# Two group-normalised 3x3 convolutions on 1024x1024 images: another chain of statistics between the passes

## The reference, cut to what matters

```
def _gn(v, G=4, eps=1e-5):            # 4 groups of 2 channels, over the whole image
    m, s = mean and var of the group
    return (g - m) / sqrt(s + eps)
x = x + conv3x3(_gn(x), L0_weight, pad=1) + L0_bias
x = x + conv3x3(_gn(x), L1_weight, pad=1) + L1_bias
```

## Time and profile before

| | |
|---|---|
| median of 3 runs | 3917.45 us (3915.92 to 3917.98) |
| profiled execution, own time | 3912.56 us |
| its span, first to last instruction | 3910.9 us |
| TensorE busy | 3472.6 us, 89% |
| ScalarE, VectorE, GpSimd busy | 44%, 37%, 15% |
| mean granted clock of TensorE | 0.969 of full |
| HBM traffic | 805 MB read, 537 MB written, 343 GB/s |

### The profile page before, as it was taken

The page is one execution under the profiler, slowest core; times in us unless marked ns, Lnnn a source line. Parts: engine busy times, 40 slices in busy tenths (PEclk is TensorE's granted clock), DMA queues, the critical chain, the costliest instruction groups (busy, mean ns, idle before and its releaser), DMA issues. The chain is left out here.

```text
span 3910.9 us, 216983 instructions
## 1 busy us (share of the span) xinstructions
PE 3472.6 (89%) x99136; PEld 1837.6 (47%) x99136; DVE 1430.8 (37%) x2460; ACT 1711.4 (44%) x1553; POOL 592.4 (15%) x1061
## 2 busy tenths in 40 slices
PE   0698999989899898998989989898998989999898
PEld 0354545445454454544445445454544445455454
DVE  7555224542245322553225432254223552223300
ACT  0243444434444343444444434444444435444444
POOL 0111111111111111111111111111111111111111
PEclk9998999999999999999999989999999989999999
DMA  9698999989989898998989989899898989999798
GB/s 344 241 385 300 404 375 337 363 302 414 354 334 359 315 415 298 385 349 334 409 293 391 337 341 415 296 390 344 349 395 296 382 308 388 387 281 309 250 312 269
DMA packets 334124, 1344.32 MB, mean 344 GB/s; under 512 B 38800, under 2 KB 38928, under 8 KB 301200
## 3 DMA queue, kind: packets, MB, share of 16 engines
q10 hardware_dynamic: 149648, 537.60, 40.7%
q0 software_dynamic: 147456, 536.94, 35.2%
q1 hardware_dynamic: 36864, 268.45, 18.2%
HBM read 805.45 MB, written 536.87 MB: 343 GB/s over the span
## 5 line engine op out<-in xcount | busy, mean ns | idle before, releaser
L391 PE MATMUL conv<-x_tile,wts 32*32 32x512 f32 x49152 | 3382.9, 601 | 138.2 <-DVE bias L541 17.1
L396 PE MATMUL conv<-x_tile,wts 32*32 32x512 f32 x49152 | 3405.2, 603 | 2.4 <-issue 2.4
L391 PEld LDWEIGHTS conv<-x_tile,wts 32*32 32x32 f32 x49152 | 1597.8, 103 | 1681.4 <-issue 1368.1
L330 ACT ACTIVATE out_tile<-conv,bias 128x1024 f32<-128x1024 f32 x512 | 570.7, 1115 | 1960.7 <-PE conv L396 1946.7
L455 DVE BATCH_NORM_STATS2 bn_mid<-out_tile 128x6 f32<-128x512 f32 x1024 | 658.8, 685 | 963.8 <-ACT out_tile L330 711.9
L396 PEld LDWEIGHTS conv<-x_tile,wts 32*32 32x32 f32 x49152 | 958.5, 103 | 78.5 <-issue 3.5
L447 DVE BATCH_NORM_STATS2 bn_x<-stat_tile 128x6 f32<-128x512 f32 x896 | 550.2, 679 | 963.0 <-DMA stat_tile<-x_dram 963.0
L334 ACT ACTIVATE out_tile<-conv,bias 64x1024 f32<-64x1024 f32 x512 | 569.1, 1111 | 13.3
L332 ACT ACTIVATE out_tile<-conv,bias 64x1024 f32<-64x1024 f32 x512 | 567.1, 1108 | 13.2
L232 POOL DMA_DIRECT2D mid_dram<-out_tile x512 | 272.9, 533 | 1538.9 <-ACT out_tile L330 1051.6
L232 POOL DMA_DIRECT2D out_dram<-out_tile x512 | 268.1, 524 | 1558.4 <-ACT out_tile L330 1086.7
(11 more groups left out here) (45 smaller groups left out, 115.1 us busy)
## 6 DMA issues: line engine op xcount, KB each, us to landing
stat_tile<-x_dram SPq DMA_DIRECT2D x256, 1024.0 KB, 9.7
mid_dram<-out_tile POOLq DMA_DIRECT2D x512, 512.0 KB, 8.5
out_dram<-out_tile POOLq DMA_DIRECT2D x512, 512.0 KB, 9.1
x_tile<-x_dram ACTq DMA_DIRECT2D x504, 512.0 KB, 12.1
x_tile<-mid_dram ACTq DMA_DIRECT2D x504, 512.0 KB, 11.8
x_tile<-x_dram ACTq DMA_DIRECT2D x8, 480.0 KB, 6.7
x_tile<-mid_dram ACTq DMA_DIRECT2D x8, 480.0 KB, 6.1
x_tile<-pad_row ACTq DMA_DIRECT2D x16, 32.0 KB
```

Source lines behind the costliest of these rows:

```text
L330: act.activation(out_tile[:, slot, 0], conv[:, parity, 0], ACT.Identity, bias=bias[:, 0:1]).then_inc(evicted, 1)
L391: nc.tensor.matmul(columns_of(parity, i, q, c), wts[part, MAIN, kw], rows_of(TILE * q, TILE, slot, c, kw), start=first, stop=end)
L396: last = nc.tensor.matmul(columns_of(parity, i, q, 1 - c), wts[part, ABOVE, kw], rows_of(TILE * above, TILE, slot if q else (slot - 1) % S ...
```

## The change

The statistics of the last two units of layer 0 (`LATE = 2`) are read straight from PSUM instead of from the evicted tiles (`take_mid_late`). The aggregate of mid is split: the first 30 units are aggregated when unit 30 begins, only the last two units' 8 parts afterwards, and the bias is added to their mean. The sum over partitions for mid is made per partition's own group, by two matmuls with the weights `sum_parts` beside the one for x, so that layer 1 needs neither `picked` nor a reduction. Both sums, x's and mid's, are issued in every pass. The 24 bias matmuls become one 128x128 matmul with the constant `sum_taps`, and `plain` goes. `wts` is made in one instruction. The pads are written by ScalarE (`begin`), around the root. GpSimd's pad row waits for `wts_ready`. The aggregate of x is moved from the start of a pass to right behind the last tile of x. ScalarE waits in the last two units of layer 0 for `second_taken` before it evicts the second block. In the setup, two small loads, two reductions and 32 small GpSimd instructions are added.

```
@@ constants, set up once @@
+OF_MID, OF_BIAS = GROUPS, GROUPS + 1
-MID_PARTS = UNITS * 2 * HALVES
+PARTS = UNITS * 2 * HALVES
+LATE = 2
+LATE_PARTS = LATE * 2 * HALVES
+SPLIT_AT = (0, PARTS - LATE_PARTS, PARTS)
+SHARES = (1 - LATE / UNITS, LATE / UNITS)
...
-        ident = sb("ident", [P, 2, TILE])
+        ident = sb("ident", [P, 2, KW, TILE])
+        of_layer = sb("of_layer", [P, 2])
+        sum_parts = sb("sum_parts", [P, 2, P])
+        sum_taps = sb("sum_taps", [P, P])
@@ gpsimd: setup, and the pad row of a pass @@
+            for late in range(2):
+                alone(pool.tensor_scalar(sum_parts[:, late], same_group[:, :], SHARES[late], 0.0,
+                                         ALU.mult, ALU.add))
+            pool.wait_ge(tap_sums, 2)
+            for layer in range(2):
+                part = slice(TILE * layer, TILE * layer + CH)
+                for r in range(ROWS):
+                    alone(pool.tensor_scalar(sum_taps[part, CH * r:CH * (r + 1)], tap_sum[part, :],
+                                             -1.0, 0.0, ALU.mult, ALU.add))
...
-                        pool.wait_ge(mean_known, 2 * n + (g // UNITS + 1))
+                        pool.wait_ge(wts_ready, 2 * n + (g // UNITS + 1))
@@ scalar: evict, and the beginning of a pass @@
                 act.activation(out_tile[:, slot, 0], conv[:, parity, 0], ACT.Identity,
                                bias=bias[:, 0:1]).then_inc(evicted, 1)
+                if layer == 0 and u >= UNITS - LATE:
+                    act.wait_ge(second_taken, LATE * n + (u - (UNITS - LATE) + 1))
...
+            def begin(n, layer):
+                p = 2 * n + layer
+                act.wait_ge(mean_known, p + 1)
+                act.activation(x_tile[:, :, 0:SIDE + 2:SIDE + 1], ones[:, :, :], ACT.Identity,
+                               scale=own_mean[:, 0:1])
+                act.wait_ge(var_read, p + 1)
+                columns = 1 if layer else GROUPS
+                act.activation(root[:, 0:columns], var[:, 0:columns], ACT.Sqrt).then_inc(root_done, 1)
+                part = slice(P - TILE, P)
+                act.wait_ge(above_known, p + 1)
+                act.sem_inc(rows_asked)
+                act.wait_ge(head_loaded, 16 * (p + 1))
+                act.activation(x_tile[part, LAST_SLOT, 1:SIDE + 1], head[part, :], ACT.Identity,
+                               bias=above[part, 0:1], scale=is_first[part, 0:1]) \
+                   .then_inc(pads_written, 1)
+                act.wait_ge(wts_ready, p + 1)
...
-                    act.wait_ge(var_read, 2 * n + (layer + 1))
-                    act.activation(root[:, :], var[:, :], ACT.Sqrt).then_inc(root_done, 1)
-                    act.wait_ge(wts_ready, 2 * n + (layer + 1))
+                    begin(n, layer)
@@ tensor: sums @@
-                nc.tensor.matmul(conv[:, 0, 0, 0:GROUPS], average[:, :], share[:, :], start=True,
-                                 stop=True).then_inc(mean_summed, 1)
+                nc.tensor.matmul(conv[:, 0, 0, 0:GROUPS], average[:, :], mv_x[:, :, 0], start=True,
+                                 stop=True)
+                for late in range(2):
+                    last = nc.tensor.matmul(conv[:, 0, 0, OF_MID:OF_MID + 1], sum_parts[:, late],
+                                            mv_mid[:, late, 0:1], start=(late == 0),
+                                            stop=(late == 1))
+                last.then_inc(mean_summed, 1)
...
-                for j in range(QUARTERS):
-                    for kind in (MAIN, ABOVE):
-                        for kw in range(KW):
-                            last = nc.tensor.matmul(
-                                conv[TILE * j:TILE * (j + 1), 0, 0, GROUPS:GROUPS + 1],
-                                plain[0:TILE, kind, kw], taken[0:TILE, :],
-                                start=(kind == MAIN and kw == 0), stop=(kind == ABOVE and kw == KW - 1))
-                last.then_inc(bias_summed, 1)
+                nc.tensor.matmul(conv[:, 0, 0, OF_BIAS:OF_BIAS + 1], sum_taps[:, :], taken[:, :], start=True,
+                                 stop=True).then_inc(bias_summed, 1)
@@ vector @@
+            def take_mid_late(n, u):
+                dve.wait_ge(conv_done, units_through(n, u))
+                for i in (1, 0):
+                    if i == 0:
+                        last.then_inc(second_taken, 1)
+                        dve.wait_ge(evicted, evicts_through(n, u, 1))
+                    for h in range(HALVES):
+                        last = dve.bn_stats(bn_mid[:, (2 * u + i) * HALVES + h, :],
+                                            conv[:, u % 2, i, h * BANK:(h + 1) * BANK])
+                last.then_inc(mid_taken, 1)
...
+            def var_shares_mid():
+                after_all(dve.tensor_copy(own_mean[:, :], conv[:, 0, 0, OF_MID:OF_MID + 1]))
+                wait_for_all()
+                dve.sem_inc(mean_known)
+                after_all(dve.tensor_scalar(shift[:, 0:2], mv_mid[:, :, 0], own_mean[:, 0:1], None,
+                                            ALU.subtract))
+                wait_for_all()
+                after_all(dve.tensor_tensor(shift[:, 0:2], shift[:, 0:2], shift[:, 0:2], ALU.mult))
+                wait_for_all()
+                dve.tensor_tensor(share_mid[:, :], shift[:, 0:2], mv_mid[:, :, 1], ALU.add) \
+                   .then_inc(var_share, 1)
...
+                if layer:
+                    after_all(dve.tensor_tensor(own_rstd[:, :], rstd[:, 0:1], newton[:, 0:1], ALU.mult))
+                else:
+                    after_all(dve.tensor_tensor(rstd[:, :], rstd[:, :], newton[:, :], ALU.mult))
+                    wait_for_all()
+                    after_all(dve.tensor_tensor(picked[:, 1], own_group[:, :], rstd[:, :], ALU.mult))
+                    wait_for_all()
+                    after_all(dve.tensor_reduce(own_rstd[:, :], picked[:, 1], AX_X, ALU.add))
+                wait_for_all()
+                dve.scalar_tensor_tensor(taken[:, :], own_mean[:, :], own_rstd[:, 0:1],
+                                         of_layer[:, layer:layer + 1], ALU.mult, ALU.mult) \
+                   .then_inc(taken_known, 1)
+                dve.scalar_tensor_tensor(wts[:, :, :, :], band[:, layer], own_rstd[:, 0:1],
+                                         ident[:, :, :, :], ALU.mult, ALU.add)
...
                 for g in range(2 * UNITS):
-                    if g == UNITS:
+                    if g < UNITS - LATE:
+                        take_mid(n, g)
+                    elif g < UNITS:
+                        if g == UNITS - LATE:
+                            dve.wait_ge(mid_taken, UNITS * n + (UNITS - LATE))
+                            dve.sem_inc(sums_begun)
+                            aggregate_mid(0)
+                        take_mid_late(n, g)
+                    if g == UNITS - 1:
                         dve.wait_ge(mid_taken, UNITS * n + UNITS)
                         dve.sem_inc(sums_begun)
+                        after_all(aggregate_mid(1))
+                        wait_for_all()
+                        dve.tensor_tensor(mv_mid[:, 1, 0:1], mv_mid[:, 1, 0:1], bias[:, :], ALU.add) \
+                           .then_inc(mean_share, 1)
                         sums_of(n, 1)
```

More of the change, by code:

```diff
@@ L208, in _ @@
                 for kind, moved in ((MAIN, CH), (ABOVE, -3 * CH)):
-                    alone(pool.affine_select(ident[part, kind], one[part, :], [[-1, TILE]],
+                    alone(pool.affine_select(ident[part, kind, 1], one[part, :], [[-1, TILE]],
                                              ALU.is_equal, 0.0, moved, 1))
@@ L216, in _ @@
                                      ALU.is_ge, 0.0, 3 * CH - 1, -1))
+            for layer in range(2):
+                part = slice(TILE * layer, TILE * (layer + 1))
+                alone(pool.affine_select(of_layer[part, layer:layer + 1], one[part, 0:1], [[0, 1]],
+                                         ALU.is_ge, 0.0, CH - 1, -1))
             pool.wait_ge(setup_loaded, SETUP)
@@ L247, in _ @@
             act.dma_start(same_group[:, :], group_sums[:, 0, :]).then_inc(setup_loaded, 16)
+            for layer in range(2):
+                act.dma_start(taps_in[TILE * layer:TILE * layer + CH, :],
+                              taps[layer].rearrange("c k t -> c (k t)")).then_inc(setup_loaded, 16)
             act.sem_inc(evicted, FREE)
@@ new lines, in aggregate_mid, with aggregate_x, var_shares_x @@
+            def aggregate_mid(late):
+                return dve.bn_aggr(mv_mid[:, late, :], bn_mid[:, SPLIT_AT[late]:SPLIT_AT[late + 1], :]
+                                   .rearrange("p a b -> p (a b)"))
+            def aggregate_x():
+                for g in range(GROUPS):
+                    last = dve.bn_aggr(mv_x[:, g, :], bn_x[:, g * PER_GROUP:(g + 1) * PER_GROUP, :]
+                                       .rearrange("p a b -> p (a b)"))
+                return last
+            def var_shares_x():
```

(44 more changed lines are left out.)

117 lines of the change are left out of this document (42 added, 75 removed).

## The result

| | before | after |
|---|---|---|
| median | 3916.68 us (3911.84 to 3917.98, 4 runs) | 3849.75 us (3844.09 to 3859.57, 4 runs) |
| ratio | | 0.9829, 95% interval 0.9815 to 0.9844 |
| profiled execution | 3912.56, span 3910.9 | 3844.09, span 3842.5 |

What follows compares the result with a forecast made beforehand. It took the chain of sums between passes, where nothing is convolved, as what costs time, hardly late rows. Savings of 53.2 + 11.4 + 1 = 65.6 us from 3912.6 gave 3847.0, with 4.9 for the median 3851; range 3832 to 3877.

Steps and rivals of the forecast that it cites:

- the mean's sum: Change of layer, share end to reading the sum: 0.74 us before, 0.9 more for added matmuls, read at 4.91 us.
- Statistics from PSUM: Change of layer: two `bn_stats` pairs no longer wait for evictions and take 2.61 us, 1.29 a pair as from SBUF.
- Aggregate: Change of layer: the remaining 48 numbers take 0.32 us; the other 720 (3.4 us) move to unit 30, hidden in 11.3 free.
- Added sum matmuls: Change of layer: two more matmuls before the mean's and the variance's sum, 0 to 1.12 us more each, taken as 0.9.
- Newton step: Change of layer, behind the reciprocal: 1.12 us, with the pad row waiting for `wts_ready` and two 0.20 us steps gone.
- Bias sum: Before the bias read: one bias matmul at 0.74 us, where the 48 instructions took 2.12 us.
- Change of image: Between images, root to bias read falls from 4.60 us, saving 1.63 us seven times, 11 us.
- The sum: Whole kernel: 53.2 + 11.4 + 1 = 65.6 us saved.
- the changes of layer: Eight changes of layer: bias read at 9.95 us instead of 16.60, saving 6.65 us each, 53 us.
- the start: First pass: 1.8 us of added matmuls in the open, 5.02 us before against 2.48 behind the reciprocal, about 1 us saved.
- Rival 1: Transfers take back the gain at seven changes of layer, as rows come later: 46.6 us, time 3898; chance 0.07.

Runs made afterwards that it cites:

- k1: Changed kernel with the statistics of units 30 and 31 taken from the evicted tiles again instead of from PSUM: 3869.39 us, 0.9887 of before.
- k2: Changed kernel with the split of the aggregate undone in time, the 120 early parts aggregated after unit 31: 3877.99 us, 0.9903 of before.
- k7: Changed kernel with TensorE's code written out for the two layers, each pass issuing only the sums it needs: 3932.18 us, 1.0042 of before.
- k5: Kernel before with one edit, GpSimd's pad row waiting for `wts_ready` instead of `mean_known`: 3907.01 us, 0.9973 of before.
- k4: Changed kernel with GpSimd's pad row starting again at `mean_known` instead of `wts_ready`: 3857.92 us, 0.9847 of before.
- k3: Changed kernel with `plain` and the loop of 24 bias matmuls put back in place of `sum_taps`: 3876.92 us, 0.9898 of before.
- k6: Changed kernel with ScalarE's images 1 to 6 written out instead of a loop: 3816.21 us, 0.9752 of before.

## Why the prediction was right

The time was forecast at 3851 and came at 3849.75, and the steps hold one by one, but for the mean's sum, which makes all that follow some 0.6 us early (us after the last matmul, at the last change of layer):

| step | forecast | measured |
|---|---|---|
| last `bn_stats` ends | 2.61 | 2.53 |
| late aggregate and bias add end | 3.27 | 3.24 |
| mean read | 4.91 | 4.34 |
| shares of the variance end | 5.79 | 5.27 |
| variance read | 7.43 | 6.86 |
| reciprocal | 7.87 | 7.29 |
| `taken` begins | 8.99 | 8.29 |
| bias read | 9.95 | 9.26 |
| pass starts | 10.8 | 10.3 |

- **Statistics from PSUM.** 2.49 us for all four, as forecast by the rows of SBUF. The 0.26 us more that the prediction worked out from the Trainium skill, VectorE: DVE Perf Modes, section on the TRN2 errata, are not there. k1 shows the part to be worth 17 to 20 us.
- **Aggregate.** 0.37 us against 0.32. The early part, 3.40 us, is covered as the 11.3 free us of the earlier trace rows said, with 2.84 us to spare; k2 shows what that cover is worth.
- **Added sum matmuls.** 0.9 us for each of the two sums was the least certain term. Share end to mean read took 1.10 here, so they cost 0.36, and 1.59 at the change of layer of image 4, so 0.85 there; the variance's took 1.59 too. The forecast held for the variance, and for the mean only where TensorE's clock had fallen (see the last section); it did not think of the clock. k7 shows 0.8 us for the sum over x that a layer-1 pass doesn't need.
- **Newton step.** Reciprocal to `taken` 1.00 against 1.12. The cause, GpSimd's pad row, is confirmed by k5 from before and by k4 from after; that it holds only single operations was not known then.
- **Bias sum.** 0.75 behind `taken`, as forecast; k3 shows 25 us.
- **Change of image.** Root to bias 2.59 against 2.72. The saving by the bias read is 1.89 us each and not 1.63, since before, the pad row held an operation there too in some of them, as the Newton or the identity step; at the first and the last change, where it held none, the saving is 1.65.
- **The sum.** 65.6 forecast, 68.4 by the spans: 59.3 against 53.2 at the changes of layer, 11.6 against 11.4 at those of image, 1.1 against 1 at the start. The miss of 6 at the changes of layer is the cheap mean sum in some (1.19 us on average from share to read, against 1.64 in the forecast, 3.6 us in all), a Newton step 0.1 shorter (1 us), and several terms under 0.1. That the median came within 2 us of the forecast is in part luck: the changes gained 6 us more than forecast, the passes took 4 back, and the runs of one kernel differ by 15.

Rival 1, the transfers take it back, fell by what the prediction named. At the change of layer of image 2, the stretch before the pass's start and its first 14 us:

```profile
1283.00:1294.00 11.00, 3.57 (x34) 3.07 (x46) 6.99 (x23) 5.08 (x6) 2.25 (x3) 0.68 0.94 358
1294.00:1308.00 14.00, 13.70 (x371) 6.99 (x352) 8.38 (x14) 3.33 (x3) 2.77 (x3) 0.88 0.80 303
```

In the kernel before, the burst ended ahead of the pass's start (0.96, then 0.23). Now it reaches into the pass (0.94, then 0.80), and it ends there without a late row: TensorE has no wait over 0.15 us between 1294 and 1339 us, and the passes' sum did not grow beyond the scatter. So the free stretch took up what was moved; what would have happened without it no run shows. The range, 3832 to 3877, holds all single runs of the changed kernel.

## What to carry to other kernels

In a chain over engines, price it link by link from a trace (release to start, not busy time), and look which wait ends last at each kind of boundary: here one kind was bound by evictions and an aggregate, the other by a jump. Move all of an aggregation but the last pieces ahead, and read those pieces from the accumulator. Before splitting a loop body by cases, count its instructions: in k7 TensorE's body, grown from one layer's to two, cost 80 us where the case it spared was worth 6.

## What the runs showed of the hardware

- **A jump back costs 4 to 6 us where the body is long.** ScalarE 4.1 to 5.2 us at five jumps (gone in k6), TensorE 6.1 us at seven (k7), and then again in the first units, some 6 us a pass. Over a body of one layer TensorE's jumps show no such wait. The page's count of instruction transfers, 6 against 110, tells the two cases apart.
- **GpSimd holds VectorE only for a moment.** One operation is stretched by 0.8 us when GpSimd's 2.8 us begin. In the kernel before a second one is held near their end (L520, 1.08 us from 3679.50, against 0.31 in k5); between them the small operations take 0.16 us and L518 0.32, as without GpSimd. The Trainium skill, SBUF — State Buffer, section on the two separate sides, says of a VectorE operation with two inputs in SBUF and a GpSimd operation that reads SBUF that whichever starts first gets the shared ports for the whole instruction and the other fully blocks. The trace differs (L561 above has two such inputs and takes 0.16 us in the midst of the pad row), and the measurement decides.
- **The clock falls within the chain.** The mean's sum begins some 3.4 us after the last convolution matmul at every change of layer, and is quicker in some than in others. Two of them in stretches (us, busy and count per engine, granted clock, DMA share, GB/s):

```profile
2216.60:2218.20 1.60, 1.41 (x6) 1.36 (x6) 0.05 (x1) 0.39 (x1) 0.48 (x1) 0.50 0.96 353
3607.30:3608.50 1.20, 0.92 (x6) 0.87 (x6) 0.09 (x2) 0.44 (x1) 0.04 (x1) 0.81 0.73 150
```

The first ran wholly at 1.2 GHz, the second mostly at 2.4. The two matmuls for mid took, in the first one's timeline, against 0.71 us above:

```profile
2217.21 0.99 PE L414 MATMUL conv<-mv_mid,sum_parts 128*128 128x1 f32 x4
```

The same shows at all sixteen changes of layer of the two profiled executions of the changed kernel: from the share to the mean read 0.98 us where the granted clock was 1.00, 1.60 where it was 0.50, and between them where it fell in the midst. So up to 0.6 us a change hang on whether TensorE's clock has fallen when the sum comes; it explains the 0.2 us between the two executions' bias reads (9.29 and 9.48), whose means for this step are 1.19 and 1.39. Where the sum comes later, the clock had always fallen: 1.60 at all changes of k1 and k2, which is 0.2 us of what each of them lost, and in the kernel before, where it came 8.9 us after the last matmul, a granted clock of 0.50 and 0.74 us from share to read at all eight. The stretch from bias read to first eviction at the changes of layer is on average the same either way, 10.1 us before and 10.0 after.
